# A head loop with sparse value lookup: drains for VectorE's own counter, and rows found three tiles ahead

## What is computed

```python
def _pk(x, Wq_pk, pk_keys):                       # 8 heads, 128 keys per half
    q = (x @ Wq_pk).reshape(b, n, P, HEADS, DIM_KEY).transpose(2, 0, 1, 3, 4)
    sim = jnp.einsum('pbnhd,pkhd->pbnhk', q, pk_keys)
    scores, idx = jax.lax.top_k(sim, 16)          # of each half
    index = idx[0][..., :, None] + 128 * idx[1][..., None, :]
    score = scores[0][..., :, None] + scores[1][..., None, :]
    final_scores, pk_idx = jax.lax.top_k(score.reshape(...), 16)
    return softmax(final_scores), take_along_axis(index.reshape(...), pk_idx)
q = (x @ Wq).reshape(b, n, HEADS, DIM) * DIM ** (-0.5)
kv_scores, indices = _pk(x, Wq_pk, pk_keys)
k = einsum('bnhk,bnhkd->bnhd', kv_scores, keys_table[indices + head * 16384])
v = einsum('bnhk,bnhkd->bnhd', kv_scores, values_table[indices + head * 16384])
out = causal_softmax(q @ k.T) @ v                 # per head
return out.reshape(b, n, HEADS * DIM) @ Wo
```

## Time and profile before

| what | value |
|---|---|
| median of the runs | 3127.12 us (3123.65 to 3127.17) |
| span of the profiled execution | 4087.1 us |
| its own time beside the span | none is given |
| instructions | 30985 |
| head loop: first gather to the end of the last | 398.4 to 4035.2 us |
| GpSimd busy | 2019.0 us (49%) |
| VectorE busy | 2320.4 us (57%) |
| TensorE busy | 1677.6 us (41%) |
| ScalarE busy | 748.5 us (18%) |
| mean granted TensorE clock | 0.633 |
| moved by gathers | 268.57 MB in 98304 packets |

### The profile page before, as it was taken

How to read it: one execution, slowest core, us unless ns; L and a number is a source line. 1 busy time by engine, 2 the same in 40 slices (tenths; PEclk the granted TensorE clock), 3 DMA queues, 4 the chain that set the end, 5 groups by cost and what they waited for, 6 DMA issues and landing times. The chain is left out here.

```text
span 4087.1 us, 30985 instructions
## 1 busy us (share of the span) xinstructions
PE 1677.6 (41%) x7360; PEld 1258.2 (31%) x7360; DVE 2320.4 (57%) x8139; ACT 748.5 (18%) x1761; POOL 2019.0 (49%) x2061
## 2 busy tenths in 40 slices
PE   4666233443344334343343434343334334343345
PEld 3656122332233223232222222232223223232224
DVE  5687555566555656466554665455545555456554
ACT  3656011121111111111111111110111111111112
POOL 0000665646555466546555465546545465545553
PEclk8878556675666556665666556665667556665567
DMA  3200222222222222222222222222222222222221
GB/s 104 78 1 9 85 81 74 84 58 81 76 77 74 65 81 80 73 59 84 77 72 78 65 81 76 73 66 82 72 68 69 65 81 77 83 59 78 73 80 52
DMA packets 107936, 291.19 MB, mean 71 GB/s; under 512 B 34080, under 2 KB 39712, under 8 KB 105760
## 3 DMA queue, kind: packets, MB, share of 16 engines
q0 software_dynamic: 98304, 268.57, 22.9%
q1 hardware_dynamic: 8496, 20.97, 1.5%
q10 hardware_dynamic: 1008, 0.33, 0.1%
HBM read 288.69 MB, written 1.05 MB: 71 GB/s over the span
## 5 line engine op out<-in xcount | busy, mean ns | idle before, releaser
L242 POOL DMA_INDIRECT ring<-table,rows x2048 | 2017.2, 985 | 2015.3 <-POOLq L240 1391.6
L654 DVE SCALAR_TENSOR_TENSOR acc<-ring,wgt,acc 128x256 f32<-128x256 f32 x1792 | 807.1, 474 | 37.1 <-DVE best L593 11.5
L1189 PE MATMUL ps<-pts,work 128*128 128x128 f32 x2176 | 459.8, 380 | 508.7 <-PEq L1187 256.9
L1189 PEld LDWEIGHTS ps<-pts,work 128*128 128x128 f32 x2176 | 412.2, 283 | 563.4 <-issue 561.7
L1161 PE MATMUL ps<-work,qT 128*128 128x512 f32 (+3 forms) x576 | 360.7, 774 | 121.6 <-issue 78.2
L1175 PE MATMUL ps<-ident,work 128*128 128x128 f32 x1088 | 240.9, 375 | 375.0 <-PEq L1170 170.9
L661 DVE TENSOR_REDUCE nmax<-ps 128x1 f32<-128x128 f32 (+15 forms) x128 | 164.9, 1288 | 305.7 <-DVEq L660 259.3
L1175 PEld LDWEIGHTS ps<-ident,work 128*128 128x128 f32 x1088 | 184.3, 196 | 436.7 <-issue 436.7
L971 ACT ACTIVATE pts<-ps 128x512 f32<-128x512 f32 (+2 forms) x320 | 167.0, 533 | 822.3 <-ACTq L970 635.5
L669 DVE RECIPROCAL prec<-psum_row 128x1 f32<-128x1 f32 x127 | 19.7, 155 | 500.1 <-DVEq L668 472.1
L1197 PE MATMUL ps<-wo,oT 128*128 128x128 f32 x256 | 85.4, 430 | 445.5 <-issue 213.3
(11 more groups left out here) (196 smaller groups left out, 2997.4 us busy)
## 6 DMA issues: line engine op xcount, KB each, us to landing
ring<-table,rows POOLq DMA_INDIRECT x2048
staged<-adj_in SPq DMA_DIRECT2D x16, 1024.0 KB, 4.8
wpkq<-w_pkq SPq DMA_DIRECT2D x8, 128.0 KB
out<-xs SPq DMA_DIRECT2D x1, 832.0 KB, 4.4
keyd<-pk_keys SPq DMA_DIRECT2D x16, 32.0 KB
wo<-w_o SPq DMA_DIRECT2D x8, 64.0 KB
out<-xs SPq DMA_DIRECT2D x1, 192.0 KB, 2.1
watt<-w_att ACTq DMA_DIRECT2D x1, 64.0 KB, 5.6
```

The source lines that it names most:

```text
L242: nc.gpsimd.indirect_dma_start(ring[:, t % RING, k, :], None, table_d, bass.IndirectOffsetOnAxis(ap=rows[:, t % RING, k:k + 1], axis=0),). ...
L654: v.scalar_tensor_tensor(a, row, w, a, ALU.mult, ALU.add).then_inc(dve_done, c.one())
L1189: ins = m.matmul(ps[:, 1, 0:P], kv[:, j, D:2 * D], pts[:, (parity + b) % 2, j % 4 * P:(j % 4 + 1) * P], start=(j == 0), stop=(j == t))
```

## The change

It does five things. (1) AHEAD = 3: in step t VectorE searches the rows of tile t+3 instead of t+2, and weighs tile t+2 instead of t+1; ScalarE and TensorE move `exp_best` and `project` one tile further ahead with it, and a third `find_all` stands ahead of step 0. (2) In the head loop no VectorE instruction raises `dve_done`, and no wait names it. (3) In their place stands `v.drain()` (as `settle()`), fourteen in a step, between groups: one part of the search and one pair of sums. (4) The sixteen sums end ahead of `find_best_index` and the look-ups, so that `slot_free` and `add_sums(t)` come ahead of L610. (5) The first half of the `bposf` copy (L607) goes ahead of `find_best_index`; `weigh` and `add_out` are cut in two parts, so that one drain serves several.

```diff
+AHEAD = 3
...
+            def settle():
+
+                v.drain()
...
             def find_best_index(t):
-                v.max_index(bpos[:, 8:16], best[:, t % 2, 8:16], candr[:, :]).then_inc(dve_done, c.one())
+                v.tensor_copy(bposf[:, 0:8], bpos[:, 0:8])
+                v.max_index(bpos[:, 8:16], best[:, t % 2, 8:16], candr[:, :])
 
             def look_up_1(t):
-                v.tensor_copy(bposf[:, :], bpos[:, :]).then_inc(dve_done, c.one())
+                v.tensor_copy(bposf[:, 8:16], bpos[:, 8:16])
...
+            def sum_pair(t, k):
+
+                sum_rows(t, k)
+                sum_rows(t, k + 1)
...
             def step(h, t, first, last):
-                a = (t + 2) % T
-                find = not (last and t >= T - 2)
+                a = (t + AHEAD) % T
+                find = not (last and t >= T - AHEAD)
...
                 if find:
                     find_start(a)
-                dve.wait_ge(dve_done, c.n)
+                settle()
                 if find:
                     find_replace(a)
-
+                if out:
+                    add_out_1((t - 2) % T)
                 dve.wait_ge(gathered[t % RING], h * (16 * TOPK * (T // RING)) + 16 * TOPK * (t // RING + 1))
-                sum_rows(t, 0)
-                n1 = sum_rows(t, 1)
...
+                sum_pair(t, 0)
+                settle()
+                if out:
+                    add_out_2((t - 2) % T)
...
-                dve.wait_ge(dve_done, n1 - 2)
                 if find:
                     find_second(a)
-                dve.wait_ge(dve_done, n1 - 1)
-                n2 = sum_rows(t, 2)
-                dve.wait_ge(dve_done, n1)
-                n3 = sum_rows(t, 3)
+                sum_pair(t, 2)
                 if prev and (t - 1) % T < 8:
                     score_max((t - 1) % T)
+                settle()
...
+                sum_pair(t, 14)
+                settle()
+
+                dve.sem_inc(slot_free, 1)
                 if find:
-                    dve.wait_ge(dve_done, n12)
                     find_best_index(a)
...
+                    settle()
                     look_up_1(a)
...
                 if t > 0:
                     add_sums(t)
+                if find:
+                    settle()
+                    look_up_2(a)
+                    settle()
+                    look_up_3(a)
+                    settle()
+                    look_up_4(a)
+                    settle()
+                    look_up_5(a)
...
-            find_all(0)
-            weigh(0)
-            find_all(1)
...
+            for t in range(AHEAD):
+                find_all(t)
+                if t < AHEAD - 1:
+                    weigh_1(t)
+                    v.drain()
+                    weigh_2(t)
...
             def step(t, first, last):
-                if not (last and t >= T - 1):
-                    exp_best((t + 1) % T)
-                if not (last and t >= T - 3):
-                    project_out((t + 3) % T)
+                if not (last and t >= T - AHEAD + 1):
+                    exp_best((t + AHEAD - 1) % T)
+                if not (last and t >= T - AHEAD - 1):
+                    project_out((t + AHEAD + 1) % T)
...
             def step(t, first, last):
-                if not (last and t >= T - 3):
-                    project((t + 3) % T)
+                if not (last and t >= T - AHEAD - 1):
+                    project((t + AHEAD + 1) % T)
```

More of the change, by code:

```diff
@@ L557, in find_start @@
                 dve.sem_inc(bank0_free, 1)
-                for p in range(2):
-                    v.max(half[:, p, 0, 0:8], sim[:, s, p * NKEY:(p + 1) * NKEY]).then_inc(dve_done, c.one())
+                v.max(half[:, 0, 0, 0:8], sim[:, s, 0:NKEY])
+                v.max(half[:, 1, 0, 0:8], sim[:, s, NKEY:2 * NKEY])
             def find_replace(t):
@@ L631, in find_all @@
[L631 to L645 removed]
+                v.reciprocal(wrec[:, t % 2:t % 2 + 1], wsum[:, t % 2:t % 2 + 1])
@@ L651, in sum_rows @@
                 if k < 2:
-                    v.tensor_scalar(a, row, w, None, ALU.mult).then_inc(dve_done, c.one())
-                else:
-                    v.scalar_tensor_tensor(a, row, w, a, ALU.mult, ALU.add).then_inc(dve_done, c.one())
-                return c.n
+                    return v.tensor_scalar(a, row, w, None, ALU.mult)
+                return v.scalar_tensor_tensor(a, row, w, a, ALU.mult, ALU.add)
             def score_max(t):
@@ L679, in step @@
             def step(h, t, first, last):
-                a = (t + 2) % T
-                find = not (last and t >= T - 2)
+                a = (t + AHEAD) % T
+                find = not (last and t >= T - AHEAD)
                 prev = not (first and t == 0)
-                if t == T - 2 and find:
-                    v.tensor_scalar(hoff[:, :], hoff[:, :], float(NKV), None, ALU.add).then_inc(dve_done, c.one())
+                out = not (first and t < 2)
+                weigh = not (last and t >= T - AHEAD + 1)
@@ L693, in step @@
-                n1 = sum_rows(t, 1)
-                if not (first and t < 2):
-                    add_out((t - 2) % T)
+                sum_pair(t, 0)
+                settle()
+                if out:
+                    add_out_2((t - 2) % T)
                 if t == 1:
                     add_sums(0)
-                dve.wait_ge(dve_done, n1 - 2)
                 if find:
                     find_second(a)
-                dve.wait_ge(dve_done, n1 - 1)
-                n2 = sum_rows(t, 2)
@@ L770, in step @@
-                dve.wait_ge(dve_done, c.n)
-                dve.sem_inc(slot_free, 1)
                 if t > 0:
                     add_sums(t)
+                if find:
+                    settle()
+                    look_up_2(a)
+                    settle()
+                    look_up_3(a)
+                    settle()
+                    look_up_4(a)
+                    settle()
+                    look_up_5(a)
                 if last and t == T - 1:
+                    settle()
@@ L796, in _ @@
                     step(h, t, False, False)
-                dve.wait_ge(dve_done, c.n)
-                dve.sem_inc(dve_done, -c.n)
-                c.n = 0
             for t in range(T):
                 step(HEADS - 1, t, False, True)
-            add_out(T - 2)
+            add_out_1(T - 2)
+            v.drain()
+            add_out_2(T - 2)
             score_max(T - 1)
-            dve.wait_ge(proj_full, 1)
-            dve.sem_inc(proj_full, -1)
-            v.reciprocal(prec[:, 3:4], psum_row[:, 3:4]).then_inc(dve_done, c.one())
-            dve.wait_ge(dve_done, c.n)
+            add_out_1(T - 1)
+            v.drain()
             v.scalar_tensor_tensor(xs[:, T - 1, :], ps[:, 1, P:2 * P], prec[:, 3:4], xs[:, T - 1, :],
@@ L998, in _ @@
             project_out(2)
+            exp_best(1)
+            project_out(3)
             for t in range(T):
```

130 lines of the change are left out of this document (44 added, 86 removed).

## The result

| | kernel before | changed kernel |
|---|---|---|
| median | 3126.29 us (3123.65 to 3127.17, 4 runs) | 3145.04 us (3144.22 to 3146.55, 4 runs) |
| profiled execution, its own time | none given for the one of the earlier trace rows; 3125.54 us for a later one | 3144.22 us |
| its span | 4087.1 us; 3123.6 us for the later one | 3142.3 us |

The ratio is 1.0065 [1.0051, 1.0079]: the change makes the kernel 0.6% slower, 18.75 us. About 1.9 us lie around a span.

A forecast was written before the change was run, and what follows sets the result against it. The prediction took GpSimd's issue of gathers to bound the kernel. Its terms, -15.6 us for late rows and +1.4 us for drains, gave -14.2 us, so 3113 us from 3127, range 3062 to 3160 us.

The forecast's parts named there:

- 51 us left over: Whole kernel: the median of 3127 us less the rebuilt 3076 us, put down to contention or GpSimd waiting for rows.
- the first of its two readings: GpSimd's gathers: contention with VectorE makes a tile's gathers take longer, 21.45 us instead of 20.0 beside one free step.
- Step 1: Head loop, rows three tiles ahead: GpSimd no longer stops for late rows; gain 15.6 us, ends 0 and 51 us.
- GpSimd was already full: Rival, GpSimd's issue: contention alone can fill the remainder, so no gain; 3124 to 3131 us, chance 0.32.
- Step 2: Ahead of the loop: a third search before step 0 lies under the first tile's gathers and costs 0.
- Steps 3 and 4: VectorE's head loop: dropping the counter gives -1.5 us in some steps, fourteen drains cost 1.8 us per step; +1.4 us in total.
- On the path: 0: Head loop: the drains add nothing to GpSimd's path; only 0.9 us in the tail and 0.5 us in the first search.
- Step 5: Head loop, sums before look-ups: add_sums and slot_free come some 3 us earlier, gating only VectorE; 0.
- The gathers get slower: Rival, GpSimd's gathers: drains spread VectorE's work so every tile costs 21.45 us; 3184 us, +57, chance 0.23.
- a tile mean above 21.05 us: GpSimd's gathers per tile: the mean from which the slower-gathers case was to be decided.
- a gather mean of 1.05 us or more: Single gathers on GpSimd: a sign that the forecast was wrong and the kernel slower.

The follow-up runs named there:

- g2: The kernel before with one row gathered per tile instead of sixteen, counter kept; 2550.28 us.
- e1d: The changed kernel with rows found two tiles ahead instead of three, drains and new order kept, fourth run, short kind; 3161.88 us, ratio 1.0101.
- g1: The changed kernel with one row gathered per tile instead of sixteen; 2731.38 us.
- e8: The kernel before with a drain in place of each VectorE wait on its own counter, nothing else moved; 3229.15 us, ratio 1.0327.
- e1: The changed kernel with rows found two tiles ahead instead of three, first run, long kind; 4131.13 us, ratio 1.0057.
- r1: The changed kernel itself, unaltered, run again in a group of the long kind; 4151.01 us, ratio 1.0184.
- e3: The changed kernel with sums 12 to 15 put back one by one between the last search parts and the look-ups; 4148.58 us, ratio 1.007.
- e3b: The changed kernel with sums 12 to 15 back in the old order, run a second time; 4101.74 us, ratio 1.0033.

## Why the prediction was wrong

**What bounds it: right.** GpSimd's issue of gathers bounds both kernels. The prediction rebuilt the median as 398 + 2638 + 40 us and had 51 us left over. They are mostly contention, the first of its two readings: the gaps were 623.5 us (620.4 in the earlier trace rows), the gathers 2060.8 us for 2017.2, 43.6 us more, and the rest is in the first stretch and around the span. With one gather a tile a step takes 16.5 us, 4.5 us under a tile's 21.0; "about 3.5 us of air per tile" was near.

**Step 1 failed: "Gain: 6.8 us in 56 intervals, scaled to 128, is 15.6 us."** Seven of the 56 intervals behind the earlier trace rows were over 20 us, and I took them for the kernel's. They belonged to the long kind of execution: in g2, where VectorE's own pace sets the interval, none is over 20 us. In the profile of the kernel before at 3125.54 us there is no wait for rows after the first tile, so there was nothing for a third tile to remove; the value was the lower of the two ends that the step gave, 0. The rival "GpSimd was already full" had this right. Behind the step stands a misreading in its first paragraph, that 960 us "belong to the recorded execution alone": the profiled execution of the changed kernel took 3144.22 us, as its other runs did (3144.64 to 3146.55), and in the long groups the kernel before took 4057 to 4121 us in the median of 7 to 29 runs. Recording costs nothing that can be seen. The rule I set, to use only stretches where nothing stalls, was broken in counting late steps.

**The third tile did help, by another way.** Between e1d and the changed kernel it is worth 17 us, near the 15.6 us of the step by luck: some 11 us are thirteen gathers that no longer start at the head of the multiply, 6 us are the difference of two executions, and GpSimd's idle time is the same.

**Step 2 held**, a third search ahead of the loop: the first gather starts at 400.37 us for 401.08.

**Steps 3 and 4: right that VectorE is not the bound, wrong on what the drains cost it, and wrong on the path.** The counter was taken to give back about 1.5 us in some steps and the drains to cost 1.8. Measured together, with the pairing and the split copy, they cost 1.4 us a step (g1 and g2). A step is then 17.9 us, inside the 21.1 us of a tile's gathers, so VectorE is not the bound, as the steps said. But "On the path: 0" is the second step that failed. It left out that a drain shifts the operations behind it against the gathers: drains cost 36.3 us of gather time in e1d, and e8 shows the same 1024 ns with drains alone. With the 17.5 us that the third tile gave back, these are the 18.8 us on the path, where the sum had 1.4. The Trainium skill (VectorE: DVE Perf Modes, "The DRAIN you can't avoid") says that a semaphore after every operation costs nothing against one at the end. No run here takes the semaphores away and puts nothing in their place, so none tests that; what the runs show is that the exchange for drains lengthened VectorE's step.

**Step 5**, sums ahead of the look-ups: 990 ns in the new order (e1, r1) and 990 and 992 ns in the old one (e3, e3b) show no effect on gathers in the long kind; drains with the old order and three tiles ahead did not run in the short one.

**The rival that came about, mis-sized.** "The gathers get slower" gave 3184 us and +57; measured were +19. Its mechanism is the one found. Its size took one tile of 21.45 us, with a gather of 1.84 us, for every tile. The mean tile is (2060.8 + 623.5) / 128 = 20.97 us before and 21.12 us after: 127 gathers already started in a compare before, for 113 after, and the two look-ups together hold no more than they did. What grew is the hold of the sums, which the rival did not name. The test that it set, a tile mean above 21.05 us, came out so; the other one, a gather mean of 1.05 us or more, was set too high, since 1015 ns against 1006 was enough. "Near 985 ns" as the mean to expect was too low for both kernels: in the long kind 994 of the kernel before's gathers start with VectorE idle, in the short kind 598.

The Trainium skill (SBUF — State Buffer, "SBUF: two separate sides") describes a lock of the port that VectorE and GpSimd share. The rows agree in kind, with gathers of 1.52 to 1.84 us beside L610 and 0.94 beside an idle VectorE, and they give the end of the hold: that of the operation in which the gather started.

The range (3062 to 3160 us) held the result, because it took most of that rival in. The sign did not come out (14 us faster forecast, 18.75 us slower measured), with 0.45 on faster and 0.23 on slower.

## What to carry to other kernels

Where GpSimd's issue of transfers is the bound, its time is set by which VectorE operations the issues start in; so split or shorten long operations with two inputs from SBUF, even if VectorE then works more (here 116 us more for 69 us less). Take waits out of an engine that has air only if they are dear: here the drains cost more than the waits they replaced, and they moved its operations against the issues. And before counting lateness in a profile, compare its span with the times of the runs; where they differ by 30%, idle time in it says nothing of the runs. Durations of single operations held (0.945 us for a free gather, 0.474 us for a sum in both kinds), but a mean over operations that are held at times did not (985 and 1006 ns).

## What the hardware showed that was not expected

- **Two kinds of execution, 30% apart.** The kernel before took 3126, 4121, 4061, 4057, 4092, and then 3127 and 3129 us in its groups; on one and the same chip it took 4057 us and, later, 3127 us, so it does not hang on the chip alone. In the long kind ScalarE and TensorE stand still for up to 24.5 and 22.6 us, VectorE for up to 6.9, with "issue" as releaser. The timeline of the kernel before in its profile of 4087.1 us, at the end of a tile's gathers:

```profile
569.05 0.63 PE L1144 MATMUL ps<-aT,wpkq 128*128 128x128 f32 x2
...
588.12 1.09 POOL L242 DMA_INDIRECT ring<-table,rows  x1 [0.31 <-issue]
...
590.10 0.28 ACT L945 ACTIVATE qpk<-ps 128x128 f32<-128x128 f32 x1 [24.46 <-issue]
...
590.69 1.19 PE L1147 MATMUL ps<-keyd,qpk 128*128 128x256 f32 x2 [21.01 <-issue]
```

  The projection was ready at 569.68, and ScalarE began to copy it at 590.10, 20.4 us later and 0.9 us after the tile's last gather ended; TensorE waited for that copy. This is one case and no rule: of the 33 such waits of ScalarE over 5 us in this profile, five ended within 3 us of the end of a tile's gathers. In the profiles of the short kind, and in g1's and g2's, no wait with "issue" as releaser is over 0.5 us on VectorE and ScalarE or over 1.3 us on TensorE's matmuls. What brings the long kind about, and whether fewer gathers would prevent it, is open: g1 and g2, with one gather a tile, ran without it in a group in which the kernel before had it, and no other number of gathers was tried there.
- **The drain's price**: 1.4 us for fourteen in a step (g1 and g2, with the pairing and the split copy in it) and 4.7 us for 29 (e8), so 0.10 and 0.16 us each over the waits that they replace. The share of either was not measured alone.
- **A held gather takes 0.81 us after the hold.** That is nearly the whole of a free one (0.945 us). Operations with one input, up to 2.29 us long, and one with its second input in PSUM hold nothing; of the two-input ones from SBUF, those of 1.05 and 0.47 us were seen to hold.
